# Layer 0 of a four-layer attention stack in another order, and eight float32 products at the start of its eight-head part

## The reference

```
layer 0:  q = Wq x + bq,  k = Wk x + bk   (32 rows each),  v = Wv x + bv  (256 rows)
          out = gamma * (v softmax(q^T k)^T) + x ;  batch norm over (batch, position)
layer 1:  group norm; one head of 256 channels; projection; x + out
layer 2:  group norm; 8 heads of 32 channels; projection; xn + out
layer 3:  group norm; 8 heads of 32 channels; projection; x + out
```

## Time and profile before

| | us |
|---|---|
| median of 3 runs | 1626.69 |
| lowest and highest | 1624.81, 1628.48 |
| the profiled execution | 1621.85 |
| its span in the trace | 1620.0 |
| PE busy in the span | 1529.4 (94%) |
| DVE, POOL, ACT busy | 1039.4, 973.7, 867.7 |

### The profile page before, as it was taken

How to read it: one execution, slowest core, us unless ns; L and a number is a source line. 1 busy time by engine, 2 the same in 40 slices (tenths; PEclk the granted TensorE clock), 3 DMA queues, 4 the chain that set the end, 5 groups by cost and what they waited for, 6 DMA issues and landing times.

```text
span 1620.0 us, 21701 instructions
## 1 busy us (share of the span) xinstructions
PE 1529.4 (94%) x8238; PEld 982.3 (61%) x8238; DVE 1039.4 (64%) x1654; ACT 867.7 (54%) x1441; POOL 973.7 (60%) x388
## 2 busy tenths in 40 slices
PE   4898979999999799999999999999999999999998
PEld 2676767888887555555555555555555556555542
DVE  3666655544544677776776776677777677777651
ACT  3544414433333266657657566656665765756663
POOL 1221211221213178787798798977878879869883
PEclk7999989999999699999999999999999999999999
DMA  4000000000000413030330321303303133042000
GB/s 169 20 20 20 1 1 0 1 1 0 20 0 15 111 46 70 10 79 11 69 79 1 79 51 48 79 1 79 72 8 79 22 83 79 1 105 63 17 27 27
DMA packets 36392, 67.53 MB, mean 42 GB/s; under 512 B 5760, under 2 KB 7872, under 8 KB 36288
## 3 DMA queue, kind: packets, MB, share of 16 engines
q1 hardware_dynamic: 36288, 66.14, 17.0%
HBM read 8.15 MB, written 4.19 MB: 8 GB/s over the span
## 4 chain that ended last, share of the span: by engine, by line
PE 59%; POOL 3%; DVE 3%; SPq 1%; issue 1%; DMA 1%; ACT 1%; DVEq 0%; ACTq 0%; POOLq 0%
PE psO L956 13%; PE psD L1029 13%; PE psD L89 12%; PE psA L1060 9%; PE psD L968 5%; PE psO L1060 5%; POOL PA L1285 3%; DVE BNS L1111 1%; SPq L1319 1%; DMA STK<-KQ 0%; DVE sums_turned L1090 0%; DVE A L1094 0%; DVE A L1096 0%; ACT PR L1244 0%; SPq L1322 0%
## 5 line engine op out<-in xcount | busy, mean ns | idle before, releaser
L1111 DVE TENSOR_REDUCE BNS<-psD 128x1 f32<-128x512 f32 x1024 | 638.2, 682 | 208.8 <-PE psD L1029 208.7
L1285 POOL TENSOR_TENSOR PA<-PA,PR 128x2048 f32<-128x2048 f32 x126 | 578.3, 4589 | 33.4 <-ACT PR L1244 18.6
L1244 ACT ACTIVATE PR<-psA 128x512 f32<-128x512 f32 x688 | 392.2, 603 | 225.5 <-PE psA L1060 203.7
L1029 PE MATMUL psD<-STK 96*128 96x512 f32 x1024 | 413.9, 410 | 12.0 <-DMA STK<-KQ 8.5
L1060 PE MATMUL psA<-STK 97*128 97x512 f32 x688 | 290.1, 423 | 3.9 <-DMA STK<-MROW 2.3
L1244 ACT ACTIVATE PR<-psO 128x512 f32<-128x512 f32 x336 | 202.2, 602 | 160.0 <-PE psO L1060 159.9
L670 POOL TENSOR_SCALAR P<-P,RS 128x1024 f32<-128x1024 f32 x64 | 71.8, 1123 | 339.2 <-DVE RS L408 339.1
L956 PE MATMUL psO<-PR,V 128*32 128x512 f32 x2048 | 246.6, 598 | 5.9 <-DVE A L1096 5.7
L1029 PEld LDWEIGHTS psD<-STK 96*128 96x128 f32 x1024 | 197.9, 193 | 65.8 <-DVE BNS L1111 16.9
L1285 POOL TENSOR_TENSOR PA<-PR 128x2048 f32<-128x2048 f32 x32 | 146.8, 4587 | 100.0 <-ACT PR L1244 100.0
L1060 PEld LDWEIGHTS psA<-STK 97*128 97x128 f32 x688 | 130.4, 190 | 111.0 <-issue 58.0
(11 more groups left out here) (148 smaller groups left out, 1927.9 us busy)
## 6 DMA issues: line engine op xcount, KB each, us to landing
STK<-KQ SPq DMA_DIRECT2D x128, 256.0 KB, 3.8
STK<-KQ SPq DMA_DIRECT2D x128, 128.0 KB, 3.7
X<-x SPq DMA_DIRECT2D x4, 1024.0 KB, 7.9
out<-X SPq DMA_DIRECT2D x3, 1024.0 KB, 6.5
XN<-w SPq DMA_DIRECT2D x2, 768.0 KB, 6.7
KH<-KL SPq DMA_DIRECT2D x8, 128.0 KB, 2.3
QH<-KL SPq DMA_DIRECT2D x8, 128.0 KB, 2.4
KQ<-w SPq DMA_DIRECT2D x1, 768.0 KB, 4.1
```

The costliest lines, as they stand in the source:

```text
L1029: mm = e.matmul(full, QS[0:STACK, group, int(u in "ae"), q, tile * PART:(tile + 1) * PART], KS[0:STACK, group, h, q, :], start=True, stop= ...
L1111: top = e.tensor_reduce(MXH[:, h, q, tile:tile + 1], full, AX.X, ALU.max)
L1244: e.activation(PR[:, J % 4, (s % QUADH) * HALF:(s % QUADH + 1) * HALF], score_bank(s, p), ACT.Exp, scale=scale).then_inc(exp_done, 1)
L1285: e.tensor_tensor(PA[:, :], PR[:, (J - 1) % 4, :] if j == 1 else PA[:, :], PR[:, J % 4, :], ALU.add).then_inc(sum_done, 1)
```

## The change

1. Layer 0, start: PE no longer waits for the constants before its first projection. The projection of batch 1 follows that of batch 0 at once, ahead of the first scores, and is gone from behind tile 1 of batch 0. The parts have two copies (KL[.., b % 2], QL[.., b % 2]). For batch 0 the three DMAs into QH are issued by ACT, those into KH by SP; for later batches SP issues all six.
2. `weigh`: part 0 waits for the low part of v0 alone, part 1 for that of v1 (before: part 0 for both).
3. Layers 0 and 1, DVE: `attended` stands behind `row_max` and `transposed_low` of its tile and not ahead of them.
4. Eight-head part, first group: ACT writes the projection to A (a buffer that is free then), the parts come from A, and the eight maxima of head 0 are float32 products of 32 rows read from A, which wait for no stack. SP fills the stacks of this group in the order of heads 1, 2, 3, 0.

```diff
-                    order = [("k", i, 0) for i in range(NQK)] + [("s", 0, 0), ("s", 1, 0)]
+                    order = [("k", i, 0) for i in range(NQK)] + ([] if L1 else [("k", 0, 1)]) + [("s", 0, 0), ("s", 1, 0)]
...
-                            if i == (5 if L1 else 1) and b + 1 < B:
+                            if i == (5 if L1 else 1) and b + 1 < B and (L1 or b):
...
-                                        e.wait_ge(stacked, 16 * STACK_DMAS * (b + 1))
+                                        e.wait_ge(stacked[b % 2], 16 * STACK_DMAS * (b // 2 + 1))
...
                                 if part == 0:
                                     e.wait_ge(t_low, NT * b + 4 * h + 4)
-                                    if h == 0:
-                                        e.wait_ge(unit_low, lows["v", 1, b])
+                                if h == 0 and part < 2:
+                                    e.wait_ge(unit_low, lows["v", part, b])
...
-                            else:
-                                e.wait_ge(s_const, 48)
                             for i in range(NQK):
                                 project(i, 0)
+                            if not L1:
+                                project(0, 1)
                             scores(0, 0)
                             scores(1, 0)
+                            if not L1:
+                                e.wait_ge(s_const, 48)
...
+                                    if i < 6:
+                                        row_max(i + 2, b)
+                                    transposed_low(i, b)
                                     if i == 6:
                                         attended(b, 0, 0)
                                     elif b and i % 2 == 0:
                                         attended(b - 1, (i + 2) // 4, (i + 2) // 2 % 2)
-                                    if i < 6:
-                                        row_max(i + 2, b)
-                                    transposed_low(i, b)
...
+                            if not L1:
+                                e.wait_ge(unit_low, lows["k", 0, 0])
+                                for dst, src in stack_copies(0, (1,)):
+                                    e.dma_start(dst, src).then_inc(stacked[0], 16)
+                                high(0, 1)
                             exponent(0, 0)
                             exponent(1, 0)
...
-                                for dst, src in stack_copies(b % 2):
-                                    e.dma_start(dst, src).then_inc(stacked, 16)
+                                for dst, src in stack_copies(b % 2, (0,) if b == 0 else (0, 1)):
+                                    e.dma_start(dst, src).then_inc(stacked[b % 2], 16)
...
+                            if P is None and q == 0:
+                                e.wait_ge(act_free, 4)
+                                e.matmul(full, A[0:CH, 1, tile * PART:(tile + 1) * PART], A[0:CH, 0, h * HALF:(h + 1) * HALF],
+                                         start=True, stop=True).then_inc(d_full, 1)
+                                return
...
-                                e.tensor_tensor(low_part(which).bitcast(F32R), low_part(which), high_part(which),
+                                e.tensor_tensor(low_part(which).bitcast(F32R), A[:, which, :], high_part(which),
...
-                            e.activation(low_part(which, mv), full, ACT.Identity, bias=bias).then_inc(act_free, 1)
+                            e.activation(A[:, which, mv] if (G, u) in ((0, "k"), (0, "q")) else low_part(which, mv), full,
+                                         ACT.Identity, bias=bias).then_inc(act_free, 1)
...
-                        for q in range(QUADH):
+                        for q in (1, 2, 3, 0) if G == 0 else range(QUADH):
```

More of the change, by code:

```diff
@@ L186, in one_head @@
                     bn_done = sem("batch_normed" + n)
[L187 to L189 removed]
+                    stacked, shifted = [sem(f"stacked{n}_{k}") for k in range(2)], sem("x_shifted" + n)
+                    order = [("k", i, 0) for i in range(NQK)] + ([] if L1 else [("k", 0, 1)]) + [("s", 0, 0), ("s", 1, 0)]
                     for b in range(B):
@@ L353, in _ @@
                                     transposes(i, b)
-                                    if not L1 and i == 1 and more:
+                                    if not L1 and i == 1 and more and b:
                                         project(0, b + 1)
@@ L517, in _ @@
                                 low(i, 0)
+                            if not L1:
+                                low(0, 1)
                             row_max(0, 0)
@@ L550, in _ @@
                                         input_low(b + 1)
-                                    if more and i == (5 if L1 else 1):
+                                    if more and i == (5 if L1 else 1) and (L1 or b):
                                         for k in range(min(2, NQK)):
@@ L591, in high @@
                                 if not L1:
-                                    wait(e, stacked, 16 * STACK_DMAS * b)
-                                hi = k_terms(i)[0] if L1 else KL[0:p, 0, :]
+                                    wait(e, stacked[b % 2], 16 * STACK_DMAS * (b // 2))
+                                hi = k_terms(i)[0] if L1 else KL[0:p, b % 2, :]
                                 bias = par("bqk1", 4)[:, i:i + 1] if L1 else par("bqk0", 1, p)
@@ L1193, in run @@
                             e.drain()
-                            e.activation(high_part(which).bitcast(F32R), low_part(which), ACT.Copy).then_inc(high_done, 1)
+                            e.activation(high_part(which).bitcast(F32R), A[:, which, :] if (G, u) in ((0, "k"), (0, "q")) else low_part(which),
+                                         ACT.Copy).then_inc(high_done, 1)
                             return
```

23 lines of the change are left out of this document (12 added, 11 removed).

## The result

The changed kernel takes 1612.42 us (median of 4 runs, 1611.11 to 1614.48); in the same sessions the kernel before took 1625.76 (4 runs, 1624.81 to 1628.48). The ratio is 0.9916 with a 95% interval of 0.9899 to 0.9934: faster, by 13.3 us. The forecast was 1612.6. That is nearer than its parts were: one gave more than forecast, three gave less, and an offset between the profiled execution and the median made up most of the rest, as the part on the prediction shows. The profiled execution of the changed kernel took 1612.07 us, of which 1610.3 us are the span.

What follows compares the result with a forecast made beforehand. Layer 0 was taken as bound by tile-to-tile hand-overs with no engine full, layer 1 by PE. Terms 0.4 - 0.4 + 6.0 + 3.3 + 4.8 = 14.1 us, off the 1626.69 us median, gave 1612.6, range 1605 to 1621.

Steps and rivals of the forecast that it cites:

- Start of layer 0: Layer 0 up to its first score: earlier projection and split stack issues gain 0.4 us, bounded mainly by DMA transfers.
- rival B: First stack in layer 0: bound by its issue after all, 2.8 us more gain, 1609.8 us; chance 10%.
- Batch 0: Layer 0's first batch: values start 1.2 us earlier but lose about 1.6 us to the low clock, together -0.4 us.
- rival A: Tiles 0 to 3 of layer 0's first batch: clock rises anyway, 5.9 us more gain, 1606.7 us; chance 12%.
- DVE's order: Layer 0's later batches: moving `attended`, with the split values' wait, shortens the tile chain by 6.0 us (4 to 8).
- the clock at tile 1: Tile 1's transposes, batches 1 to 3: shorter idle time keeps the clock up, 3.3 us gained (0 to 5.1).
- rival C: Later batches of layer 0: clock falls before tile 6 instead of tile 1, none of 3.3 us comes, 1615.9; chance 15%.
- Effect (b): Tile 6 in layer 0: `attended` behind the low part delays the next batch's first maximum, 0.63 us lost three times.
- Start of the eight-head part: Eight-head part's first group: float32 products fill the stack wait at full clock, 4.8 us gained (-0.4 to 7.6).
- Rival D: Eight-head start: 32-row products don't keep the clock up, gain -0.4 instead of 4.8 us, 1617.8 us; chance 10%.
- E: DVE's order in the tiles: each tile's delay comes back at the next, 9.3 us less gain, 1621.9; chance 5%.
- F: Eight-head start: 32-row products cost more than the narrow projection's; at 3.4 us each the kernel takes 1631.3; chance 3%.

Runs made afterwards that it cites:

- e4: Kernel before plus only the early projections, second buffer and stack issues on two queues: 1623.48 us, ratio 0.9994.
- e7: Changed kernel with loads of x for batches 2 and 3 and layer 1's weights issued behind the first stack: 1609.89 us, ratio 0.9913.
- e1: Kernel before plus only DVE's order, `attended` behind its tile's maximum and low part: 1613.09 us, ratio 0.9934.
- e2: Kernel before plus only the split values' wait, v0 waiting for its own low part: 1626.83 us, ratio 1.0002.
- e5: Changed kernel with the eight float32 products reading all 128 rows of A, altering head 0's shift: 1611.16 us, ratio 0.9924.
- e10: Changed kernel with head 0's keys copied into a zeroed 128-row tile, so the exact products read 128 rows: 1608.88 us, ratio 0.9899.
- e12: The changed kernel run again, unaltered, in a later session on another chip: 1613.02 us, ratio 0.9922.
- e6: Changed kernel with `attended` at tile 6 put back ahead of the maximum and low part: 1611.76 us, ratio 0.993.
- e3: Kernel before plus only the eight-head part, the 32-row float32 products and the stack order: 1623.6 us, ratio 0.9994.
- e9: Changed kernel with one unread 128-row matmul behind each of the eight float32 products: 1620.3 us, ratio 0.9977.

## Why the prediction was right, and where not

- **Start of layer 0** (0.4 forecast, within -1.0 to 3.2): -0.4. The reason I chose by, busy DMA engines, was right, and rival B, the issue as the bound, fell by e4 and e7. What I had priced at the low end did happen: batch 1's transfers begin at 20.00, before batch 0's stack is in, and ACT issues until 17.5 (its third issue took 1.36 us) before it turns to KL of batch 1. How the 0.4 us divide between them no run separates. (The 9.91 us of the prediction are the idle time of the weight loads; the matmuls waited 9.03.)
- **Batch 0** (-0.4): from the first score to tile 6 it gave 0.5 us (the row at 0.0 behind one at -0.4), so start and batch 0 together gave 0.0, as forecast. Up to the values 1.4 us were gained for 1.2, and from there to tile 6 1.0 lost for 1.6. The clock stayed at 1.2 GHz until 44.9, as I had expected; rival A fell.
- **DVE's order** (6.0) **and the clock at tile 1** (3.3): 10.5 us for the 9.3. By stretch: from tile 6 to the next tile 1 I had 0.82 each and measured 1.03, 1.05 and -0.18, the last with a low stretch of 1.7 us in it; from tile 1 to tile 6 of batches 1 and 2 0.95 + 1.7, measured 2.85 and 2.82; from tile 1 of batch 3 on 1.66 + 1.7, measured 2.9. The mechanism was right; e1 shows it alone. The clock's term was right in size as well: three low stretches gone and one new at tile 6 make 2 x 1.7 = 3.4 us. The wait at tile 6 did grow (to 2.46 us, not 2.7), and the clock fell there in batch 2 and not in batch 1. That is rival C in part, and by chance: over the nine traces with this wait it fell 11 times of 18. The mis-sized term is the chain, 7.1 us for 6.0. Effect (b) cost 0.4, 0.4 and nothing instead of 0.63 three times (1.1 us more), the stretches to tile 6 gave 0.2 more each, and batch 3 gave 0.45 less. The part of it that I gave to the values' wait, 1.66 us in batch 3, was right only together with DVE's order (e2), and the same edit is what lengthened the wait at tile 6: e1, without it, waits 1.57 there, kept the clock, and is 0.65 us faster from tile 6 of batch 0 to layer 1.
- **Start of the eight-head part** (4.8, ends -0.4 and 7.6): 2.6. The step that failed is "PE has no idle time between the projections and these products, so I take the full clock". PE had none, and the clock fell 2.3 us into the products. Rival D was right in its mechanism and only its size was off: two and a half products were still at the full clock, so 11.8 us and not 13.6. The stacked products start 19.06 us behind the part's first matmul, before 15.92, and up to the next projections 1.6 us were gained (27.21 for 28.83). The other 1.0 came behind them, where no term of mine stood: the clock was back 2.8 us behind their start and not 4.8. e5 and e10 show both the cause and what the products give with 128 rows in use, 4.9 us up to the projections and 5.7 to 5.8 to the real score.
- **Behind the first real score** (0 forecast): 3.1 lost. "Layer 1 and all behind the first real score unchanged in length" was wrong for the second half; I had a price for a low stretch but no term for stretches that come or go behind the place that was changed. What brings them stays open.
- **Layer 1** (0): 0.24 lost, within what other traces show without cause (289.1 to 289.8 us from its start to the eight-head part in 13 of the 14 traces). Rivals E and F fell: tile 1's wait is gone for good, and a product of 32 rows costs what the narrow projection's instructions cost, two of them 0.43 us apart at the full clock and 0.85 at the low one.
- **The sum.** 14.1 forecast, 9.7 between the two profiled executions, 13.3 between the medians. The errors in the parts sum to 4.4 us (+1.2, -0.24, -2.2, -3.1 and roundings), and the offset of before's profiled execution from its median gave 3.5 back, which is luck. So is, then, the closeness of 1612.6 to 1612.42. Before's runs in the three later sessions lay between 1619.93 and 1632.12 with medians of 1624.87, 1624.0 and 1626.96, and the intervals of after and e12 together allow a gain of 9 to 16 us. The range from 1605 to 1621 took in all of this.

## What to carry to other kernels

Before a reordering of an engine that isn't full, follow one tile's chain and see what stands ahead of the instruction that the full engine waits for: an operation that nobody waits for, moved behind, brought the next tile about 1.45 us forward, and 1.7 more where the clock had fallen in the wait, while the same move at tile 6 cost 0.4 (e1, e6). Look then at which wait grows when another is removed: the values' edit gave nothing alone (e2) and made the wait at tile 6 long enough to lose the clock in 11 of 18 places. Where 32-row products fill a wait and the clock falls in them, pad them with zeros to 128 rows (e10: 7.1 us instead of 11.8). And look at what else is in the DMA queues before splitting the issues of a late transfer: moving later loads behind it took 2.1 us off the time from issue to use, where the split gave nothing (e7, e4).

## What I had not expected of the hardware

- TensorE's granted clock fell to 1.2 GHz while PE was busy without a gap, 2.3 us (after), 3.4 us (e3) and 2.1 us (e9) into matmuls that use 32 of 128 rows. With 128 rows, even if 96 of them are zeros, it stayed at 2.4 GHz for the same 7.1 us (e5, e10). The Trainium skill ("TensorE: Matmul & The Clock Gate", section "Part 1: The HAM clock gate") says that a hardware block gates the clock by how busy PE has recently been. The traces agree only if busy means more than an instruction in flight: PE read as full in all three.
- An idle time of 2.46 us ahead of tile 6 cost the clock in one batch of after and not in another, and 11 times of 18 over all traces that have it; tile 1's 1.99 us cost it 11 times of 12 in before, e2, e3 and e4 (in e3 not in batch 1, where the transposes at 77.24 took 1.06 us, but in batch 3, 1.82 us); 1.57 us in e1 never did, in two places. Such a place can't be priced to better than the 1.7 us that one stretch costs.
- The length of an issue varies: ACT's third took 1.36 us in after and 0.61 in e7, SP's third 0.59 in after and 1.07 in e7. What lengthens one no run shows.
